# A decoder layer with routed experts: TensorE's expert loop with two tiles per turn, row buffers addressed by parity

## The reference, cut to what matters

```python
x = layernorm(x + self_attention(x))             # 8 heads, softmax over 64 keys
x = layernorm(x + cross_attention(x, ctx, mask)) # 16 heads
x = layernorm(x + experts(x))                    # 8 experts, DFF = 512, the best 2 per token
```

```python
probs = softmax(einsum('btd,ed->bte', x, Wr))
topk_vals, topk_idx = top_k(probs, 2)
router_weights = topk_vals / topk_vals.sum(-1, keepdims=True)
h = silu(einsum('btd,efd->btef', x, W1))
y = einsum('btef,edf->bted', h, W2)
out = einsum('bte,bted->btd', gate, y)           # gate holds router_weights
```

## Time and profile before

| | us |
|---|---|
| median of 3 runs (1389.78 to 1392.18) | 1391.59 |
| profiled execution, its time | 1394.73 |
| profiled execution, its span | 1392.9 |
| TensorE busy | 972.9 (70%) |
| VectorE busy | 856.7 (62%) |
| ScalarE busy | 728.6 (52%) |
| GpSimd busy | 444.5 (32%) |

### The profile page before, as it was taken

The page is one execution under the profiler, slowest core; times in us unless marked ns, Lnnn a source line. Parts: engine busy times, 40 slices in busy tenths (PEclk is TensorE's granted clock), DMA queues, the critical chain, the costliest instruction groups (busy, mean ns, idle before and its releaser), DMA issues.

```text
span 1392.9 us, 30650 instructions
## 1 busy us (share of the span) xinstructions
PE 972.9 (70%) x10082; PEld 818.1 (59%) x10083; DVE 856.7 (62%) x2598; ACT 728.6 (52%) x1364; POOL 444.5 (32%) x536
## 2 busy tenths in 40 slices
PE   4888888884999999999997205111497977677740
PEld 2777777773888878888885104000386866456530
DVE  3788888884788888888885712000254566566452
ACT  3766666663867767767664203000275755456531
POOL 3132333332010010100104273777102054554555
PEclk8998888896999999999995557555698999999985
DMA  6930000000000000000000013111133334444431
GB/s 192 289 82 15 15 15 15 15 8 20 11 11 19 9 19 9 9 19 9 0 2 1 1 47 77 55 57 51 45 93 79 90 93 100 101 105 98 98 87 53
DMA packets 157231, 73.69 MB, mean 53 GB/s; under 512 B 76034, under 2 KB 151042, under 8 KB 157188
## 3 DMA queue, kind: packets, MB, share of 16 engines
q1 hardware_dynamic: 148996, 56.34, 15.5%
q0 software_dynamic: 8192, 16.79, 4.3%
HBM read 22.76 MB, written 37.75 MB: 43 GB/s over the span
## 4 chain that ended last, share of the span: by engine, by line
PE 34%; DVE 19%; ACT 14%; another core or an unknown queue 13%; issue 12%; POOL 4%; DMA 1%; SPq 1%; DVEq 0%; ACTq 0%; POOLq 0%
PE bank L452 8%; PE bank L453 7%; PE bank L454 7%; PE bank L554 4%; DVE at L927 3%; DVE X L1004 3%; ACT XTa L748 3%; DVE mx L911 3%; ACT qzh L748 3%; PE bank L540 3%; POOL xd L414 2%; PE bank L531 2%; DVE st L994 2%; POOL wst L427 1%
## 5 line engine op out<-in xcount | busy, mean ns | idle before, releaser
L427 POOL DMA_INDIRECT wst<-yd,pos x128 | 129.3, 1011 | 218.4 <-DVE z L1119 112.6
L452 PE MATMUL bank<-XTa,qzh 128*128 128x128 f16 x768 | 146.1, 226 | 37.7 <-ACT XTa L748 37.7
L927 DVE TENSOR_TENSOR at<-bank,rc 64x32 f32<-64x32 f32 (+1 forms) x768 | 153.5, 200 | 14.4
L762 ACT ACTIVATE pr<-bank 128x512 f32<-128x512 f32 x192 | 114.0, 594 | 78.3 <-PE bank L531 77.1
L911 DVE TENSOR_REDUCE mx<-bank 128x8 bf16<-128x512 f32 x192 | 132.9, 692 | 29.0 <-PE bank L454 23.4
L833 ACT ACTIVATE pr<-bank 128x512 f32<-128x512 f32 x96 | 57.5, 599 | 178.0 <-remote 90.4
L414 POOL DMA_INDIRECT xd<-XTa,pos x128 | 123.1, 962 | 83.3 <-issue 65.1
L454 PE MATMUL bank<-XTa,qzl 128*128 128x128 f16 x768 | 146.8, 227 | 0.0
L453 PE MATMUL bank<-XTa,qzh 128*128 128x128 f16 x768 | 146.6, 226 | 0.0
L766 ACT ACTIVATE pt<-bank 128x512 f32<-128x512 f32 x192 | 113.2, 590 | 61.6 <-PE bank L540 61.2
L833 ACT ACTIVATE xs<-bank 128x512 f32<-128x512 f32 x96 | 57.4, 598 | 163.8 <-remote 101.1
(11 more groups left out here) (203 smaller groups left out, 3091.8 us busy)
## 6 DMA issues: line engine op xcount, KB each, us to landing
yd<-at SPq DMA_DIRECT2D x96, 128.0 KB
xd<-blank SPq DMA_DIRECT2D x2, 3072.0 KB, 20.7
X<-x_dram SPq DMA_DIRECT2D x16, 256.0 KB, 2.8
wst<-w_dram SPq DMA_DIRECT2D x16, 256.0 KB, 2.7
xd<-blank SPq DMA_DIRECT2D x1, 4096.0 KB, 28.6
cin<-ctx_in_dram SPq DMA_DIRECT2D x16, 256.0 KB, 2.9
out_dram<-z SPq DMA_DIRECT2D x16, 256.0 KB
xd<-blank SPq DMA_DIRECT2D x1, 2048.0 KB, 21.4
```

The costliest lines, as they stand in the source:

```text
L427: nc.gpsimd.indirect_dma_start(out=yg[k][:, t, :], out_offset=None, in_=yd[chunk_of(n)], in_offset=bass.IndirectOffsetOnAxis(ap=pos[k][:, ...
L452: nc.tensor.matmul(out_, lh, rh, start=start, stop=False, **kw)
L762: nc.scalar.activation(pr[u % 2][:], SC[u % 2][:], ACT.Exp).then_inc(s["ex"], 1)
L927: m = nc.vector.tensor_tensor(dst, src, r, ALU.mult)
```

## The change

TensorE's loop makes one turn per two tiles: 48 turns, the last written out, and one word of three expert numbers per turn (the turn's two tiles and the next one). As four row buffers are still in use, the buffer of a tile now depends on whether the turn is even or odd: the four buffers become quarters of one tensor `ct`, and TensorE forms the address of the tile's rows from a register. Four semaphores for the landing of the loads become two, one for even and one for odd tiles; so that each counts one load at a time, SyncE waits before the load of tile t+4 until tile t+2 has landed. GpSimd's wait ahead of the second chunk's scatter is for 6 halves instead of 10. ScalarE's and VectorE's loops and SyncE's order keep four tiles per turn.

```diff
-        cth = [sb(f"cth{i}", [P, GTOK], F16) for i in range(2)]
-        ctl = [sb(f"ctl{i}", [P, GTOK], F16) for i in range(2)]
+        ct = sb("ct", [P, 4 * GTOK], F16)
+        cth = [ct[:, i * GTOK:(i + 1) * GTOK] for i in range(2)]
+        ctl = [ct[:, (2 + i) * GTOK:(3 + i) * GTOK] for i in range(2)]
...
-        ld_t = [sem(f"ld_t{n}") for n in range(4)]
+        ld_t = [sem(f"ld_t{n}") for n in range(2)]
...
+            def landed(n, k):
+                wait_apart(sp, ld_t[k % 2], n * 8 + 16 - 8 * (k % 2), ld_w, 96)
...
                         wait_apart(sp, f_h, 2 * (4 * j + k) + 2, ld_w, 96)
+                        landed(4 * j + k + 2, k)
                         load(ahead, k if ahead > c else 4 * j + k + 4 - CB[c], k)
...
             for k in range(4):
+                if k >= 2:
+                    sp.wait_ge(ld_t[k % 2], 16)
                 load(0, k, k)
...
-                    pool.wait_ge(f_h, 10)
+                    pool.wait_ge(f_h, 6)
...
-            def up(k, c, base):
+            def up(k, c, base, slot):
                 n = 2 * (k % 2) + c
+                rows = [ct[:, bass.ds(slot * GTOK + h * RT, RT)] for h in range(2)]
                 for h in range(2):
                     w = base + (2 * c + h) * 2 * P
-                    m = three(H[n][:, h * RT:(h + 1) * RT], (W1[:, bass.ds(w, P)], W1[:, bass.ds(w + P, P)]),
-                              (xt[k][:, 0, :], xt[k][:, 1, :]), start=h == 0, skip_group_check=True)
+                    m = three(H[n][:, h * RT:(h + 1) * RT], (W1[:, bass.ds(w, P)], W1[:, bass.ds(w + P, P)]), rows, start=h == 0, skip_group_check=True)
                 m.then_inc(f_h, 1)
...
-            def four(j, word, last):
+            def two(j, word, last):
                 base = offset(word, 0)
-                for k in range(4):
-                    i, follow = 4 * j + k, not (last and k == 3)
+                for k in range(2):
+                    i, follow = 2 * j + k, not (last and k == 1)
                     if follow:
                         ahead = offset(word, k + 1)
-                        pe.wait_ge(ld_t[(k + 1) % 4], 16 * (j + 1 + (k + 1) // 4))
+                        slot = 2 * ((j + k) % 2) + 1 - k
+                        pe.wait_ge(ld_t[1 - k], 16 * (j + 1 + k))
                     for c in range(2):
                         if follow:
-                            up((k + 1) % 4, c, ahead)
-                        if k == 2 and c == 0 and not last:
+                            up(k + 1, c, ahead, slot)
+                        if k == 0 and c == 1 and not last:
                             pe.reg_mov(experts, load_word(j + 1))
                         down(i, k, c, base)
                     base = ahead
...
-            with pe.Fori(0, NJ - 1) as j:
-                four(j, carried(), False)
-            four(NJ - 1, carried(), True)
+            with pe.Fori(0, NW - 1) as j:
+                two(j, carried(), False)
+            two(NW - 1, carried(), True)
```

More of the change, by code:

```diff
@@ L35 @@
 NJ = NTILE // 4
+NW = NTILE // 2
 FJ = max(CB[c + 1] // 4 + 1 - CHUNKS[c][0] // GT for c in range(NC - 1))
 TAIL = NJ - FJ
-NX = 24 + P + NTILE + KS + 4
+NX = 24 + P + NTILE + KS + 2
 class Layer:
@@ L154, in program @@
         pos = [sb(f"pos{k}", [P, NT], U32) for k in range(2)]
-        tabw = sb("tabw", [P, NJ], I32)
+        tabw = sb("tabw", [P, NW], I32)
         mneg = sb("mneg", [P, GT], F32)
@@ L174, in program @@
         sl = [ql, kl] + xtl
-        xt = [q[:].rearrange("p (c r) -> p c r", c=2) for q in cth + ctl]
+        xt = [ct[:, k * GTOK:(k + 1) * GTOK].rearrange("p (c r) -> p c r", c=2) for k in range(4)]
         yb = [at[n // 2][:, 2 * (n % 2):2 * (n % 2) + 2, :] for n in range(4)]
@@ L271, in load @@
             def load(c, n, k):
-                sp.dma_start_transpose(xt[k], xd_v[c][bass.ds(n, 1)].rearrange("o r c -> (o r) c")).then_inc(ld_t[k], 16)
+                sp.dma_start_transpose(xt[k], xd_v[c][bass.ds(n, 1)].rearrange("o r c -> (o r) c")).then_inc(ld_t[k % 2], 16)
+            def landed(n, k):
+                wait_apart(sp, ld_t[k % 2], n * 8 + 16 - 8 * (k % 2), ld_w, 96)
             def store(c, n, k):
@@ L659, in load_word @@
             def load_word(j):
-                return pe.value_load(tabw[0:1, bass.ds(j, 1)], min_val=0, max_val=E ** 5 - 1)
+                return pe.value_load(tabw[0:1, bass.ds(j, 1)], min_val=0, max_val=E ** 3 - 1)
             def offset(word, k):
                 return pe.snap(word // E ** k % E * (2 * DFF))
-            def up(k, c, base):
+            def up(k, c, base, slot):
                 n = 2 * (k % 2) + c
+                rows = [ct[:, bass.ds(slot * GTOK + h * RT, RT)] for h in range(2)]
                 for h in range(2):
                     w = base + (2 * c + h) * 2 * P
-                    m = three(H[n][:, h * RT:(h + 1) * RT], (W1[:, bass.ds(w, P)], W1[:, bass.ds(w + P, P)]),
-                              (xt[k][:, 0, :], xt[k][:, 1, :]), start=h == 0, skip_group_check=True)
+                    m = three(H[n][:, h * RT:(h + 1) * RT], (W1[:, bass.ds(w, P)], W1[:, bass.ds(w + P, P)]), rows, start=h == 0, skip_group_check=True)
                 m.then_inc(f_h, 1)
@@ L702, in carried @@
             def carried():
-                return pe.snap(experts, min_val=0, max_val=E ** 5 - 1)
+                return pe.snap(experts, min_val=0, max_val=E ** 3 - 1)
             pe.wait_ge(r_tab, 1)
@@ L709, in _ @@
             for c in range(2):
-                up(0, c, offset(word, 0))
+                up(0, c, offset(word, 0), 0)
             pe.reg_mov(experts, word)
-            with pe.Fori(0, NJ - 1) as j:
-                four(j, carried(), False)
-            four(NJ - 1, carried(), True)
+            with pe.Fori(0, NW - 1) as j:
+                two(j, carried(), False)
+            two(NW - 1, carried(), True)
         @block.scalar
@@ L1086, in _ @@
                 link(nc.vector.tensor_reduce(et, past, AX.X, ALU.add))
[L1087 to L1090, removed]
+            ets = wst[0:1, 3900:3900 + NTILE + 2]
+            powers = cst[0:1, NX - 2:NX].unsqueeze(1).to_broadcast([1, NW, 2])
+            digits = wst[0:1, 3072:3072 + NTILE].rearrange("p (j k) -> p j k", k=2)
+            low_digits = wst[0:1, 3200:3200 + NW]
             link(nc.vector.memset(ets[:, NTILE:], 0.0))
             link(nc.vector.tensor_scalar(ets[:, 0:NTILE], ets[:, 0:NTILE], float(E - 1), None, ALU.min))
-            link(nc.vector.tensor_tensor(digits, ets[:, 0:NTILE].rearrange("p (j k) -> p j k", k=4), powers, ALU.mult))
+            link(nc.vector.tensor_tensor(digits, ets[:, 0:NTILE].rearrange("p (j k) -> p j k", k=2), powers, ALU.mult))
             link(nc.vector.tensor_reduce(low_digits, digits, AX.X, ALU.add))
-            nc.vector.scalar_tensor_tensor(out=tabw[0:1, :], in0=ets[:, 4:].rearrange("p (j k) -> p j k", k=4)[:, :, 0], scalar=float(E ** 4),
+            nc.vector.scalar_tensor_tensor(out=tabw[0:1, :], in0=ets[:, 2:].rearrange("p (j k) -> p j k", k=2)[:, :, 0], scalar=float(E ** 2),
                                            in1=low_digits, op0=ALU.mult, op1=ALU.add).then_inc(r_tab, 1)
@@ L1204 @@
     const[:, 2 * P + 24:2 * P + 24 + NTILE] = np.arange(NTILE)
-    const[:, 2 * P + 24 + NTILE:P + NX - 4] = np.arange(KS) * RT
-    const[:, P + NX - 4:] = E ** np.arange(4)
+    const[:, 2 * P + 24 + NTILE:P + NX - 2] = np.arange(KS) * RT
+    const[:, P + NX - 2:] = E ** np.arange(2)
     arrays = {
```

## The result

| | before | after |
|---|---|---|
| median of 4 runs each, us | 1390.82 | 1418.26 (1416.8 to 1422.96) |
| ratio | | 1.0202, interval 1.0176 to 1.0229 |
| profiled execution, its time / span | 1394.73 / 1392.9 | 1418.78 / 1417.0 |

The change makes the kernel 27 us slower by the medians, 24 us by the two profiled executions. The forecast was 47 us, 1439. In the changed kernel the lines have moved: `three` is L460 to L462 (was L452 to L454), the word load L668 (L660), the jump back L721 (L712), the scatter L422 (L414), the row load L274 (L272), `low` L1109 (L1100), silu L842 and L843.

The account below looks back on a forecast made before the run. TensorE's instruction queue was taken to limit the quiet stretch, GpSimd's DMAs the starved one. Gate -4.7 + 7.4, quiet stretch +32.2 and gather stretch +12.5 gave +47.4 us on 1391.6: 1439 us, range 1405 to 1475.

Parts of the forecast that it names:

- earlier gate and its two tiles: Second chunk's scatter released at 6 halves: GpSimd 4.7 us earlier, two tiles left for later, +7.4 us.
- quiet stretch: 996 to 1120 us, TensorE limited by its instruction queue: 38.8 tiles x 0.83 = +32.2 us.
- gather stretch: 1120 to 1346 us, 50 tiles beside gathers: two thirds of 3.3 us a turn absorbed by waits, +12.5 us.
- address: Row address formed from a register in TensorE's queue: three instructions, 0.4 us a tile, 1.6 us for four.
- The turn: Four tiles of TensorE's loop in the quiet stretch: 11.5 + 0.9 + 0.8 + 1.6 = 14.8 us.
- Word load: Load of expert numbers in TensorE's queue, one more per four tiles: +0.9 us.
- Way back: Return to the start of TensorE's loop, one more per four tiles: +0.8 us.
- A: Rival: half-size loop body needs no code fetches behind GpSimd's DMAs, TensorE no longer starved, 1316 us; chance 0.07.
- starved stretch: 861 to 996 us, TensorE does 112 matmuls while GpSimd issues 96 indirect DMAs; expected as long as before.
- B: Rival: gather stretch absorbs nothing, 1468 us, or 1486 with the dearest addresses; chance 0.12.
- C: Rival: TensorE's queue hides more, only holes at load and way back double, about 1400 us; chance 0.12.
- my own case: Main forecast, chance 0.66: 1439 us; 1418 with cheap addresses and full absorption, 1461 with dear ones and half absorbed.

Follow-up runs that it names:

- first group: Kernel before with row address from a register (1.0039), a second word load (1.0020), scatters in fours (0.9479); changed kernel with GpSimd's old wait (1.0187).
- fourth group: Kernel before with register row address and second word load together, 1401.75 us; kernel before without GpSimd's wait, 1381.12 us.
- second group: TensorE not starved: changed kernel with one more word load 1.0270, with scatters in fours 1.0144; kernel before with scatters in twos 0.9945, without GpSimd's wait 0.9875.
- the third: Changed kernel run once more, 1414.30 us; kernel before with eight tiles per turn, 1383.18 us.
- twos: Kernel before with the scatters issued two at a time, each two released by TensorE's progress: 1237.89 us, ratio 0.9945.

## Why the prediction was right in direction and too high by 20 us

Sums of the profiled executions, before to after:

| step | predicted | measured |
|---|---|---|
| ahead of the first scatter | 0 | -2.0 |
| earlier gate and its two tiles, to tile 8 | +2.7 | +1.5 |
| quiet stretch, tile 8 to 46 | +32.2 | +24.1 |
| gather stretch, tile 46 to 95 | +12.5 | +0.3 |
| behind the last tile | 0 | +0.2 |
| sum | +47.4 | +24.1 |

**What bounds it: right.** In the quiet stretch TensorE's queue is the limit. Each thing added to it (address, load, both) lengthened the turn, and the array had the same 36 matmuls a tile to do. Shown by the first and the fourth group.

**The turn: right to 3%, by terms that were not all right.** 14.8 us for four tiles were forecast, 14.45 came, and word loads 7.2 us apart stood at the low end of 7.2 to 7.6. By terms: address 1.6 forecast, 0.8 alone, with two instructions a tile more and not three. Word load 0.9, which was 0.49 alone, 0.69 on top of the address and 0.54 on top of the changed kernel's turn. Way back 0.8, and here it is 1.25 to 1.4 with all else that a second turn brings, but only 0.4 when one is taken away from the kernel before. That the array needs 10.5 of the turn's 11.5 us may be why little is gained by taking away. It doesn't explain what the additions cost: an item doesn't cost more the longer the turn is already, since the load's 0.54 us at the longest turn is less than its 0.69. A way back alone, added at a fixed length of body, wasn't tried, so the last 1.25 to 1.4 us isn't divided further and its cause stays open. The Trainium skill's compare-and-branch of about 108 ns ("Advanced Engine Details and Errata", section Control Flow Timing) fits no row: 218 ns in each of these kernels.

**The quiet stretch: mis-sized by 8 us.** The turn accounts for 38 tiles x 0.73 = 28 us. The rest is a term that the sum lacked: in this stretch stands also the first burst of eight gathers. With it a turn of the kernel before lasted 8.8 us longer than its neighbours (20.3 against 11.5), in the changed kernel 5.7 (12.9 against 7.2). Like the gather stretch, it swallowed 3 to 4 us of the slower loop. Where TensorE isn't starved the burst leaves no mark: with the first gather at 989.9 us, the turns of the changed kernel with scatters in fours stayed at 7.2 us around it. That suggests that on the other chips a run of GpSimd's gathers holds TensorE up as its scatters do; no run tests it by itself.

**The gather stretch: the step that failed.** "I take two thirds absorbed": nearly everything was. 36 us of slower queue (12.25 turns x 2.94) gave +0.3 in this pair of executions. Over all kernels of the starved kind, with quiet turns from 11.3 to 14.5 us for four tiles, this stretch took 215 to 223 us: before 221.4, after 221.7. Between kernels with the fast and the slow loop on one chip the difference was 2 us in the first group (scatters in fours 220.7, gate undone 222.7) and 5 in the third (eight tiles per turn 215.0, after 220.2), so up to 5 of the 36 us may have stayed. In the second group it was 197 to 200 for 11.6 to 15.5 us. The stretch has a length of its own, 17.6 to 18.2 or about 16 us for four tiles, and a loop shorter than that is waited for by hardly anybody. The changed kernel shows it turn by turn: between 1226.9 and 1287.7 us its jumps back come 7.2 to 7.4 and 10.4 to 10.6 us apart in alternation, one turn at the queue's own pace, the next one waiting. I had set 3.1 us of waits for VectorE against 3.3 of added queue time and took the waits for the whole reserve. They fell by 15 us only, from 34.4 to 19.1, where the loop had added some 31 in that stretch (10.7 times four tiles at 2.93); so by subtraction the other half was covered by idle time of another kind, which I had mentioned as "issue" and left out of the sum. No row divides it: TensorE's idle time named "issue" rose, from 19.4 us (1137 to 1330, before) to 28.4 (1156 to 1350, after), because it holds the added holes as well. Its largest row in each:

```profile
PE bank L452 <- issue: 11.1, 19, 1.5
...
PE bank L460 <- issue: 22.5, 46, 1.2
```

One slip besides: of 3.3 us a turn, two thirds absorbed leave 1.1 and not 1.0, which is 1 us in the sum. ScalarE, too, waits longer for TensorE without the stretch getting longer. Its waits for TensorE, 1156 to 1356 us in the changed kernel:

```profile
ACT xs L842 <- PE bank L462: 43.6, 20, 4.4
```

Over 200 us of the kernel before (1130 to 1330) it was 24.0 in 15 times. GpSimd's waits for VectorE between gathers stayed at 49.1 against 46.4 us. Gather, VectorE's sum, ScalarE's output and its store follow one another group by group, and the tile loop runs in their gaps. That this chain sets the length is what the waits suggest; no run shortened it, so it isn't shown.

**The gate: right**, to about 1 us; undone alone it changed nothing.

**The rivals.** A (the starved stretch goes away) didn't come: 134.6 us, 111 matmuls. Pacing the scatters does take the starved stretch away, and then the kernel before comes to 1319 us, where A had 1316 for the changed one. B (gather stretch absorbs nothing, 1468) was the opposite of what happened. C (costs hidden, about 1400) was wrong on the queue as a whole: loads 7.2 us apart, not under 6.2. But it was right on the load, 0.44 us against 0.49 measured, and right that the gather stretch absorbs; 1418 lies midway between C and my own case. For cheap addresses and full absorption the text had 1418, and that is the time that came; that it fits to the microsecond is chance, since the turn was longer than in that case (14.45 us for 14.0) and the burst of gathers made up for it.

**What would show it.** Held: spacing of the loads, release of GpSimd (856 forecast, 854.4), starved stretch as long, waits for VectorE well below 3 us for four tiles (1.7), no late row loads, and three to four more fused instructions a tile (3.5 over all lines, of which the addresses are two and not three). Missed: TensorE busy near 75% in the quiet stretch. It was 88% between 1082 and 1140 us:

```profile
1082.00:1140.00 58.00, 51.21 (x581) 39.34 (x579) 27.82 (x49) 34.78 (x65) 0.00 (x0) 1.00 0.28 73
```

The busy time counts each matmul to its modelled end, 0.22 or 0.27 us, and so hides part of every hole; by the pace of the starts it is 10.5 of 14.45 us, 73%.

## What to carry to other kernels

A loop's cost per turn counts only in stages where that engine's queue is last. Take each stage's own length per turn first; where a stretch takes 16 us whatever the loop does and the loop 11.5, the loop may grow by 4 us for next to nothing, and where the queue is already late, every register instruction cost 0.1 us here. If a stage runs at a small part of its speed for another reason, here 135 us beside unbroken GpSimd DMAs, then that is what to work on: a few lines of pacing gave 5%, more than any shape of the loop that was tried. Measure it on more than one chip, since on one of them the stage was not slow at all: there the wait dropped altogether gave the best time, 1229 us for 1245, and where TensorE is starved pacing in fours did, 1319 us for 1390. The kernel before in fours wasn't run on the one kind, nor twos or the changed kernel in fours on the other.

## What the runs showed of the hardware that was not expected

- TensorE beside GpSimd's unbroken indirect DMAs: 96 to 115 matmuls in 120 to 135 us in most groups, 1440 in 122 us in the second; for the kernel without the wait that is one and the same program. Four DMAs in a row cost one or two holes of about 1 us.
- In that stretch the granted clock was 0.53, about the lower of the two levels (1.2 of 2.4 GHz), where TensorE did about one matmul in a microsecond; with the scatters in fours it was 0.97. The clock alone doesn't make the stretch slow: a matmul there lasts 0.26 us and stands behind 1.92 us of idle time.
- A jump back cost TensorE's queue 218 ns by its row and left a hole of 0.65 us in the changed kernel's array, but taking every second one away from the kernel before gave only 0.4 us for each.
